# Three PSUM banks of a maximum pass used as one double and one single bank, with one VectorE reduction for each

## The reference, cut to what matters

```python
scores = jnp.einsum('bhqd,bhkd->bhqk', q, k) / math.sqrt(hd)
causal = jnp.triu(jnp.ones((S, S), dtype=bool), k=1)
scores = jnp.where(causal[None, None], -jnp.inf, scores)
attn = jax.nn.softmax(scores, axis=-1)
attn_out = jnp.einsum('bhqk,bhkd->bhqd', attn, v)
```

## Time and profile before

| | us |
|---|---|
| median of 3 runs | 2708.45 (2705.41 to 2710.56) |
| span of the profiled execution | 2663.3 |
| PE busy, all stages | 2394.4 (90%) |
| DVE busy, all stages | 2072.5 (78%) |
| ACT busy, all stages | 1463.1 (55%) |
| reductions of L883, DVE busy | 1357.2 |

### The profile page before, as it was taken

One profiled execution on the slowest core, in us unless ns is written; L12 is line 12 of the kernel. 1 busy time (PEld: TensorE's weight loads), 2 busy tenths in 40 slices (PEclk: granted clock), 3 DMA queues, 4 the chain that ended last, 5 costly groups with the idle time before them and its releaser, 6 DMA issues. The chain is left out here.

```text
span 2663.3 us, 49751 instructions
## 1 busy us (share of the span) xinstructions
PE 2394.4 (90%) x14968; PEld 1211.4 (45%) x14968; DVE 2072.5 (78%) x3856; ACT 1463.1 (55%) x1762; POOL 377.9 (14%) x319
## 2 busy tenths in 40 slices
PE   0999947999999999998899999999999868886998
PEld 0889942333333333232333333333322247776888
DVE  7888889999999988562799999988864257776776
ACT  2444513566666666777566666666677733332443
POOL 2111149500000000000000000000000023333344
PEclk9999977999999999999999999999999979998999
DMA  4122247300000021000410000003100144443232
GB/s 123 64 95 91 90 114 186 104 9 9 9 9 1 9 50 43 13 10 17 92 30 9 9 9 9 1 9 70 28 9 9 22 115 126 126 126 97 64 95 71
DMA packets 158629, 144.79 MB, mean 54 GB/s; under 512 B 36448, under 2 KB 142176, under 8 KB 158304
## 3 DMA queue, kind: packets, MB, share of 16 engines
q1 hardware_dynamic: 155360, 133.94, 18.9%
q0 software_dynamic: 3072, 8.39, 0.9%
HBM read 95.61 MB, written 46.66 MB: 53 GB/s over the span
## 5 line engine op out<-in xcount | busy, mean ns | idle before, releaser
L883 DVE TENSOR_REDUCE attn_MX<-psB 128x1 f32<-128x512 f32 (+3 forms) x2352 | 1357.2, 638 | 352.5 <-PE psB L756 223.2
L869 ACT ACTIVATE attn_PB<-psB 128x1024 f32<-128x1024 f32 (+3 forms) x1152 | 1035.8, 950 | 563.9 <-PE psB L788 509.7
L756 PE MATMUL psB<-attn_KS,attn_QS 96*128 96x512 bf16 (+3 forms) x2352 | 764.5, 370 | 51.5 <-DVE attn_MX L883 44.9
L788 PE MATMUL psB<-attn_QS,attn_KS 104*128 104x512 bf16 (+3 forms) x2304 | 652.6, 363 | 24.5 <-ACT attn_QS L846 16.0
L803 PE MATMUL psB<-attn_PB,attn_V 128*32 128x512 f32 (+3 forms) x4608 | 579.8, 570 | 0.0
L756 PEld LDWEIGHTS psB<-attn_KS,attn_QS 96*128 96x128 bf16 x2352 | 200.6, 97 | 639.8 <-DVE attn_MX L883 522.2
L788 PEld LDWEIGHTS psB<-attn_QS,attn_KS 104*128 104x128 bf16 x2304 | 210.2, 98 | 336.1 <-ACT attn_PB L869 128.9
L1043 POOL TENSOR_TENSOR W1L<-W,W1H 128x512 fp32r<-128x512 f32 x36 | 53.8, 1524 | 1664.3 <-ACT W1H L1120 1664.3
L803 PEld LDWEIGHTS psB<-attn_PB,attn_V 128*32 128x32 f32 x4608 | 96.3, 108 | 175.9 <-issue 166.8
L759 PE MATMUL psB<-attn_mask_qk,attn_idb 128*128 128x128 bf16 x544 | 119.2, 227 | 0.0
L42 PE MATMUL ps_experts<-W2H,HH_experts 128*128 128x256 f32 x256 | 83.9, 328 | 35.1 <-DVE Y_experts L1233 20.3
(11 more groups left out here) (213 smaller groups left out, 3216.5 us busy)
## 6 DMA issues: line engine op xcount, KB each, us to landing
W<-in_w SPq DMA_DIRECT2D x18, 1024.0 KB, 5.5
attn_KS<-qk_parts SPq DMA_DIRECT2D x240, 64.0 KB, 3.7
attn_QS<-qk_parts SPq DMA_DIRECT2D x210, 64.0 KB, 2.8
qk_parts<-proj_PT SPq DMA_DIRECT2D x32, 384.0 KB, 3.3
attn_V<-v_rows SPq DMA_DIRECT2D x40, 256.0 KB, 4.8
v_rows<-proj_VA SPq DMA_DIRECT2D x32, 256.0 KB, 2.0
XI_experts<-rows_by_place SPq DMA_DIRECT2D x9, 512.0 KB, 6.3
AO_experts<-attention_sums SPq DMA_DIRECT2D x9, 512.0 KB, 6.7
```

Of the source, the lines that this page charges most:

```text
L756: mm = nc.tensor.matmul(ps[:, bank, 0:width], QS[0:MROW, i % 4, h, j * P:(j + 1) * P], KS[w][0:MROW, h, kc * CH:kc * CH + width], start=Tr ...
L788: mm = nc.tensor.matmul(ps[:, bank, r * P:CH], KS[w][0:KROWS, h, kb * P:(kb + 1) * P], QS[0:KROWS, i % 4, h, r * P:CH], start=True, stop=( ...
L869: nc.scalar.activation(PB[:, u % RING, 2 * pair:2 * pair + 2, r * P:CH], ps[:, 2 * (s % 2):2 * (s % 2) + 2, r * P:CH], ACT.Exp, scale=HD * ...
L883: nc.vector.tensor_reduce(MX[:, m % 4, HG * j + h, kc:kc + 1], ps[:, MB + off % 3, 0:w], AX.X, ALU.max).then_inc(reduced, 1)
```

## The change

Jobs are grouped. A new function cuts a step's jobs into groups of one or two; a group with an even number may hold two neighbouring jobs (of one key chunk; in the diagonal chunk also of one query tile, so that their widths agree), a group with an odd number holds one. It takes the largest number of pairs that leaves an even number of groups in a step. Banks 5 and 6 serve the even groups, bank 7 the odd ones. A group waits until the group two before it has been reduced, PE raises `maxed` once per group, and DVE reduces a group with one instruction, over one or two banks, into one or two neighbouring columns. The pace counts a group at the cost of its jobs together, and the quarters and halves within a unit are now counted in groups.

```diff
+def reductions(jobs, c):
+    def split(pairs):
+        out, at = [], 0
+        while at < len(jobs):
+            j, h, kc = jobs[at]
+            two = len(out) % 2 == 0 and pairs > 0 and at + 1 < len(jobs) and jobs[at + 1][2] == kc and (kc < c or jobs[at + 1][0] == j)
+            pairs -= two
+            out.append(jobs[at:at + 1 + two])
+            at += 1 + two
+        return out
+
+    return next(found for pairs in reversed(range(len(jobs) + 1)) if len(found := split(pairs)) % 2 == 0)
...
-    cost = [(TPC if kc < steps[m % LS][1] else j + 1) / TPC for m in range(LS + AHEAD) for j, _, kc in jobs[m % LS]]
+    cost = [sum((TPC if kc < steps[m % LS][1] else j + 1) / TPC for j, _, kc in group) for m in range(LS + AHEAD) for group in jobs[m % LS]]
...
-    jobs = [[(j, h, kc) for kc in range(c + 1) for j in range(TPC) for h in range(HG)] for _, c in steps]
+    jobs = [reductions([(j, h, kc) for kc in range(c + 1) for j in range(TPC) for h in range(HG)], c) for _, c in steps]
...
                     if used is not None:
                         pe.wait_ge(reduced, used)
-                    bank = MB + off % 3
...
+                    for n, (j, h, kc) in enumerate(group):
...
+                        bank = MB + (n if off % 2 == 0 else 2)
...
                     mm.then_inc(maxed, 1)
...
-                        max_job(0, m, n, job, n - 2 if n > 2 else None, 96)
+                        max_job(0, m, n, job, n - 1 if n > 1 else None, 96)
...
-                                max_job(g + m // LS, m, at, jobs[m % LS][n], g * J_PER + at - 2, 96 * (LS // 4 * g + m // 4 + 1))
+                                max_job(g + m // LS, m, at, jobs[m % LS][n], g * J_PER + at - 1, 96 * (LS // 4 * g + m // 4 + 1))
...
-                def reduce_job(m, off, need, job):
-                    j, h, kc = job
+                def reduce_job(m, off, need, group):
+                    j, h, kc = group[0]
                     w = CH if kc < steps[m % LS][1] else P * (j + 1)
+                    at, n = HG * j + h, len(group)
+                    bank = MB + (0 if off % 2 == 0 else 2)
                     dve.wait_ge(maxed, need)
-                    nc.vector.tensor_reduce(MX[:, m % 4, HG * j + h, kc:kc + 1], ps[:, MB + off % 3, 0:w], AX.X, ALU.max).then_inc(reduced, 1)
+                    nc.vector.tensor_reduce(MX[:, m % 4, at:at + n, kc:kc + 1], ps[:, bank:bank + n, 0:w], AX.X, ALU.max).then_inc(reduced, 1)
```

More of the change, by code:

```diff
@@ L743, in _, with max_job @@
             def _(pe):
-                def max_job(reads, i, off, job, used, q_need):
-                    j, h, kc = job
+                def max_job(reads, i, off, group, used, q_need):
                     w, c = steps[i % LS]
[L748 to L752, removed]
                     if used is not None:
                         pe.wait_ge(reduced, used)
-                    bank = MB + off % 3
[L756 to L759, removed]
+                    for n, (j, h, kc) in enumerate(group):
+                        width = CH if kc < c else P * (j + 1)
+                        if h == 0 and j == 0 and kc == 0:
+                            pe.wait_ge(q_in[i % 4], q_need)
+                        if h == 0 and j == 0:
+                            pe.wait_ge(kv_in[w][kc], 112 * (reads + 1))
+                        bank = MB + (n if off % 2 == 0 else 2)
+                        mm = nc.tensor.matmul(ps[:, bank, 0:width], QS[0:MROW, i % 4, h, j * P:(j + 1) * P],
+                                              KS[w][0:MROW, h, kc * CH:kc * CH + width], start=True, stop=(kc < c))
+                        if kc == c:
+                            mm = nc.tensor.matmul(ps[:, bank, width - P:width], idb[:, :], mask_qk[:, :], start=False, stop=True)
                     mm.then_inc(maxed, 1)
```

## The result

The changed kernel takes 2868.4 us (2860.3 to 2869.1), against 2708.5 us before: a ratio of 1.058 (95% interval 1.056 to 1.060), 160 us slower. The forecast was 2813 us, the range 2755 to 2870. (In the description of the kernel before, the loop over two passes is line 815 and the loop over units line 827.)

A forecast was written before the change was run, and what follows sets the result against it. The prediction took PE to be the bound, issuing without a gap, with DVE second and 6% to spare. Terms of 66 + 5 + 20 + 10 + 4 = 105 us on 2708 gave 2813 us, range 2755 to 2870 us.

The forecast's parts named there:

- units A and B: Common attention units: A double, single, PV, double; B single, double, PV, single; a pair takes 6.42 us, before 5.93.
- a double that costs like two: Rival: a merged two-bank reduction lasts 1.37 us, same waits but larger, 106 in place of 66 us: 2855 us, chance 0.08.
- the prologue: Ahead of the loop, 48 jobs in 24 us: refills at half speed lengthen it by 4 us (0 to 8).
- The double: One reduction over two banks in the maximum pass, forecast to last 1.217 us.
- The paced units: Common attention units: PE waits for bank refills, 0.50 us a pair, 132 pairs, 66 us.
- the units with other groupings: Other attention units with jobs, about 55 a pass: 0.05 us of wait each, 5 us (0 to 12).
- The diagonal rush: Diagonal jobs at a step's end: two slots in place of three, 0.6 us over 32 steps, 20 us (0 to 35).
- The rival of the falling clock: Rival: the granted clock falls to 0.91 over 1200 us of paced units, about another 100 us: 2915 us, chance 0.05.
- The order and the larger rush: At step ends: two or three more jobs in about six steps of a pass, 10 us (0 to 20).
- The 45 us outside the span: Starting point: the profile's 2663.3 us span against the runs' 2708.45 us median, so some 45 us lie outside.
- fewer instructions win: Rival: DVE's time decides in the maximum pass and banks come free early, 44 us go: 2664 us, chance 0.05.

## Why the prediction was right, and where its sum was wrong

*The sign and the mechanism* were right. PE was the bound, DVE's time could be saved almost without effect (208 us less of it brought 28 us), and the double's refill put PE into waits. The walk of units A and B gave 6.42 us and the trace has 6.46; the waits were put at 0.17 and 0.38 us and are 0.17 and 0.4. Of the 0.04 us, half is the double's 1.226 us and half the way back to PE: a double that starts at 731.43 ends at 732.66 us, PE starts at 732.71, and 0.04 us had been used for it.

*The size* was not, and that the range still held the result is partly luck. The sum was 105 us and the loss is 160. The measured 2868.4 us lie 19 us above the end that the forecast's own bounds give (2849) and less than 2 us below the end of the range, which had been put wider for a double that costs like two. No double did. By experiment the terms are 87 us off the diagonal where 71 and a part of the prologue's 4 stood, 48 in the diagonal where 20 stood, and 26 for the order where 10 stood.

*The double.* 1.217 us forecast, 1.226 measured. By the Trainium skill's formula ("VectorE: DVE Perf Modes", the section on the TRN2 errata) an estimate gives 1.192 us; the trace stays above that, by 34 ns for a double and 26 for a single, so the price from rows was the better one.

*The paced units.* With the measured 0.53 us, 132 pairs come to 70 us (forecast 66). The doubles off the diagonal cost 87 us by experiment, against 66 + 5 and a share of the prologue. Some 15 us are left. They may lie in the units with other groupings, to which I gave 0.05 us each, but these weren't measured singly.

*The diagonal rush* is the term that was mis-sized: 20 us forecast, 48 us measured on top of the rest and 62 alone, above even the bound of 35. Two things were missing. I asked about the clock only for the paced units, where it stayed at 1.00 (the windows from 700 and from 750 us). It fell in some of the rushes, where PE waits most, and that may be up to 38 of the 48 us. And I priced the slots one by one and let scores and PV cover a part, though the covers wait in the same queue; what this alone is worth is argued, not measured. The rival of the falling clock had the right cause in the wrong place, and at 0.05 for the whole stage it had no share in the sum.

*The order and the larger rush:* 10 us stood for the rush and nothing for the order; together they cost 26.

*The prologue:* 4 us forecast. From its first reduction to the end of its maxima it takes 32 us (410.35 to 442.44) in place of 26 (412.72 to 438.70), 6 us more and inside the bounds.

*The 45 us outside the span* don't exist. In every other kernel's profiled run the device time is about 2 us above the span, and the rest was the standstill that the profiled run missed. The sum was one of differences, so nothing hung on it, but I took a wrong reading for granted.

*The rivals.* That fewer instructions win is refuted: with fewer instructions the kernel is 160 us slower, two instructions in place of one account for 31 us at the same depth, and 208 us less of DVE's busy time in the kernel before bring 1%. That a double costs like two is refuted by its 1.226 us. The Trainium skill's rule to minimize the count of operations ("VectorE: DVE Perf Modes", rules for kernel authors) stands there for chained operations, which these reductions are not. It points the right way for DVE's own time, as the 31 us show, but here it was paid for with depth.

## What to carry to other kernels

When you merge two instructions that free buffers, write down the cycle: length of the merged instruction, signal, refill, start. Compare it with the work that is left to cover it. Here 0.69 us of handshake stood against 0.60 us of cover. The time to signal and refill counts beside the work itself: one buffer less of depth cost 210 us with no instruction changed. Price the short stages too, and look at PE's granted clock there, not only where most of the time goes.

## What was not expected of the hardware

An unbroken row of 32 indirect DMAs on GpSimd, one every 1.28 us, holds DVE for 34 us in all (up to 19 us at once) where each alone, some 10 us apart, leaves no gap above 0.8 us beside it in the stretch shown. It costs 36 to 40 us of this kernel, and it is absent from one profiled run that has the same row. What it is that the other engines lack in that time, the traces don't say beyond "remote" and "issue".

PE's clock fell within a rush of about 13 us, though PE is busy for 92% of the 50 us around it (45.91 of 50.00, clock 0.86). The busy share gave no sign of it; the granted clock did.
